# Convolution, top-k token attention and write-back on one core: scatters ordered by image, a semaphore for each image, and the way back two slots sooner

## The reference, cut to what matters

```
xn   = x normalised over each (image, channel) plane
y    = conv 7x7, dilation 5, 32 channels -> 1, of xn, then an affine batch norm
imp  = sigmoid(gelu(y))                      # one value for each pixel
idx  = sorted indices of the 192 largest imp of each image
xs   = xn * imp
tok  = xs at the 192 pixels + position code  # 192 x 32 for each image
t2   = attention (8 heads) + layernorm + feed-forward + layernorm of tok
xs at the 192 pixels := t2
out  = x + xs
```

## Time and profile before

| what | us |
|---|---|
| median of 3 runs (lowest, highest) | 1260.27 (1259.71, 1261.93) |
| profiled execution | 1271.68 |
| its span | 1269.9 |
| PE busy | 962.1 |
| DVE busy | 836.7 |
| ACT busy | 791.3 |
| POOL busy | 615.8 |

### The profile page before, as it was taken

How to read it: one execution, slowest core, us unless ns; L and a number is a source line. 1 busy time by engine, 2 the same in 40 slices (tenths; PEclk the granted TensorE clock), 3 DMA queues, 4 the chain that set the end, 5 groups by cost and what they waited for, 6 DMA issues and landing times.

```text
span 1269.9 us, 21613 instructions
## 1 busy us (share of the span) xinstructions
PE 962.1 (76%) x6440; PEld 739.8 (58%) x6440; DVE 836.7 (66%) x2116; ACT 791.3 (62%) x1938; POOL 615.8 (48%) x845
## 2 busy tenths in 40 slices
PE   1297686678978888888888888887777688488647
PEld 1175564467756665776577666765655466376434
DVE  7143677657856876688778777876677468455523
ACT  1154464457646776677768677867577578478535
POOL 1032332661466366645764475548444663671532
PEclk9599797889989999999999999999889589789855
DMA  9379896855666789878997899776645456447768
GB/s 213 103 229 261 222 266 180 226 127 147 160 154 155 193 229 255 211 214 245 254 234 206 244 246 246 188 208 178 160 109 147 122 123 192 135 118 217 206 186 272
DMA packets 181225, 246.89 MB, mean 194 GB/s; under 512 B 70742, under 2 KB 77142, under 8 KB 181110
## 3 DMA queue, kind: packets, MB, share of 16 engines
q1 hardware_dynamic: 170613, 238.46, 69.3%
q10 hardware_dynamic: 2304, 4.65, 1.7%
q0 software_dynamic: 8192, 2.40, 1.5%
HBM read 123.61 MB, written 121.80 MB: 193 GB/s over the span
## 4 chain that ended last, share of the span: by engine, by line
PE 38%; DVE 18%; issue 11%; DMA 10%; POOL 9%; ACT 8%; SPq 5%; DVEq 0%; POOLq 0%; ACTq 0%
PE cv L541 9%; PE sc L660 6%; PE tr L575 5%; PE pp L673 4%; PE xb L525 4%; PE ms L689 3%; DMA flat<-imp_flat 3%; DVE junk L1133 3%; DVE res L1337 2%; PE ib L588 2%; ACT wgt L855 2%; SPq L351 2%; POOL tok_x L1023 2%; POOL tok_imp L1023 2%; POOL tok_pos L1023 2%
## 5 line engine op out<-in xcount | busy, mean ns | idle before, releaser
L541 PE MATMUL cv<-X,w_conv 128*128 128x330 f32 (+1 forms) x1024 | 300.0, 417 | 19.1 <-POOL X L997 16.9
L855 ACT ACTIVATE wgt<-ib,eps_col,mom 128x440 f32<-128x440 f32 (+1 forms) x256 | 176.9, 697 | 170.2 <-PE ib L588 161.7
L1337 DVE SCALAR_TENSOR_TENSOR res<-tr,mom,wgt 128x440 f32<-128x440 f32 (+1 forms) x192 | 122.7, 644 | 174.9 <-PE tr L575 165.1
L541 PEld LDWEIGHTS cv<-X,w_conv 128*128 128x128 f32 x1024 | 188.2, 200 | 53.2 <-issue 20.1
L1041 POOL TENSOR_SCALAR res<-res,mom 128x440 f32<-128x440 f32 (+1 forms) x152 | 93.4, 617 | 230.3 <-DVE res L1337 229.2
L525 PE MATMUL xb<-cst,X 128*110 128x128 f32 x900 | 150.5, 293 | 71.3 <-ACT xt L821 51.0
L660 PE MATMUL sc<-k_b,qm 128*128 128x192 f32 x768 | 170.1, 346 | 13.5 <-ACT pr L884 5.9
L821 ACT COPY xt<-xb 110x512 f32<-110x512 f32 x225 | 130.6, 581 | 66.7 <-DMA table<-xt 35.2
L525 PEld LDWEIGHTS xb<-cst,X 128*110 128x110 f32 x900 | 103.5, 141 | 97.9 <-ACT xt L821 56.2
L1133 DVE TENSOR_SCALAR_CACHE_REDUCE junk<-flat,th 128x379 bf16<-128x379 f32 x200 | 120.2, 601 | 54.0 <-ACT th L841 53.4
L575 PE MATMUL tr<-cst,rt 110*128 110x110 f32 x720 | 112.0, 283 | 54.7 <-issue 38.0
(11 more groups left out here) (176 smaller groups left out, 1559.0 us busy)
## 6 DMA issues: line engine op xcount, KB each, us to landing
table<-xt SPq DMA_DIRECT2D x240, 224.0 KB
rt<-table SPq DMA_DIRECT2D x240, 224.0 KB, 4.7
out<-res SPq DMA_DIRECT2D x320, 137.5 KB
X<-in_x SPq DMA_DIRECT2D x58, 412.5 KB, 5.8
X<-in_x SPq DMA_DIRECT2D x58, 343.8 KB, 5.3
conv_rows<-cvr SPq DMA_DIRECT2D x64, 188.0 KB
y<-conv_rows SPq DMA_DIRECT2D x64, 165.4 KB
out<-res SPq DMA_DIRECT2D x64, 68.8 KB
```

Of the source, the lines that this page charges most:

```text
L541: last = mm(cv[:, 0:CUT[half]], w_conv[:, 4 * q + z], X[:, m % XI, at0:at0 + CUT[half]], start=z == 0, stop=z == 3)
L855: last = A(wgt[:, n % 2, at0:at0 + w], ib[:, at0:at0 + w], ACT.Identity, scale=mom[:, NB * g + b, 2:3], bias=eps_col[:, 1:2])
L1337: last = v.scalar_tensor_tensor(res[:, first + at0:first + at0 + w], back_bank(g, u)[:, at0:at0 + w], mom[:, NB * g + b, 0:1], wgt[:, n % ...
```

## The change

Three things are changed. The two scatters that POOL issues in one slot are now those of one image (k = b and k = 4 + b), in the order of the images, and each image has its own semaphore `scat[b]`, raised by 16 by each of two DMAs. The load of unit 0 waits for image 0's only, and the loads of the first units that hold rows of images 1, 2 and 3 (7 and 8, 15, 22 and 23) for theirs; the other readers wait for all four. And BACK is SCORES + 40 = 127 instead of 129, so that every instruction of the way back, with its loads, the parts of the importance and the output stores, stands two slots sooner against the rest, and the whole schedule has two slots fewer.

```diff
-        scat = raised("scat", 1, 8 * 16)
+        scat = [raised(f"scat{b}", 1, 2 * 16) for b in range(NB)]
...
-        SCATTER, BACK = SCORES + 36, SCORES + 42
+        SCATTER, BACK = SCORES + 36, SCORES + 40
         IMPB = (BACK - 3, BACK + 1, BACK + 9, BACK + 16)
...
                 n = U * g + u
-                if u == 0:
-                    sp.wait_ge(scat, upto(scat, g))
+                for b in range(NB):
+                    if 4 * max(u - 1, 0) // RQ < b <= (4 * u + 3) // RQ or u == b == 0:
+                        sp.wait_ge(scat[b], upto(scat[b], g))
...
-            def scatter(g, part):
+            def scatter(g, b):
                 pool.wait_ge(t2_ok, upto(t2_ok, g))
-                for k in range(2 * part, 2 * part + 2):
+                for k in (b, NB + b):
                     gp.indirect_dma_start(table[g], bass.IndirectOffsetOnAxis(ap=idx[:, g % 2, 0, k:k + 1], axis=0),
-                                          rb[:, k, :], None).then_inc(scat, 16)
+                                          rb[:, k, :], None).then_inc(scat[b], 16)
...
                 if g >= 2:
-                    dve.wait_ge(scat, upto(scat, g - 2))
+                    for b in range(NB):
+                        dve.wait_ge(scat[b], upto(scat[b], g - 2))
...
                     if g:
-                        dve.wait_ge(scat, upto(scat, g - 1))
+                        for b in range(NB):
+                            dve.wait_ge(scat[b], upto(scat[b], g - 1))
```

## The result

The changed kernel took 1249.52 us (median of 4 runs, 1245.91 to 1252.68) against 1261.1 for the kernel before (1259.71 to 1271.67). The ratio is 0.9864, interval 0.9828 to 0.9899: 1.36% faster, some 17 us, where 9.3 us (0.74%) had been forecast. Two later repeats gave 0.9872 (0.9832 to 0.9911) and 0.9849 (0.9817 to 0.9881). So the direction was right and the size was not. The median of 1249.52 by itself lies inside the range, and the medians of the first runs are only 11.6 apart; but they are of four runs each, and executions of one kernel spread by 10 us and more (e4, the same kernel: 1243.80 to 1257.67).

What follows compares the result with a forecast made beforehand. No engine was taken to bound the whole; the tail was a block of DMA work starting at SP's release. -7.3 + 1.0 - 3.5 + 0.5 = -9.3 us, from 1260.27 to 1251.0 us; range 1245.9 to 1259.5.

Steps and rivals of the forecast that it cites:

- First image's semaphore, end of the last group: End of last group: SP released after the second scatter instead of the eighth, gain 7.3 us (ends 0 and 7.34).
- the store of block 11: End of last group: SP reaches this output store at 1217.3, POOL's unit is finished at 1217.0, so it just fits.
- Two slots fewer: Two more units of work come before the last group's last scatter: +1.0 us (ends 0 and 2).
- The rotation: Middle: the way back's loads move to the quiet slot, the flat load lands sooner: -3.5 us (half of 7.05).
- The new waits: SP's scatter waits: covered in groups 0 to 3, tight in group 6: +0.5 us (ends 0 and +3.2).
- The rule weighed there: SP's traffic can hold up an image's own semaphore; group 6 would pay 3.2 us, making the sum -6.6.
- Rival B: Only the end gains, the flat load waits as before: -5.8 us, 1254.5 us; chance 0.27.
- C: Rival: the end doesn't gain, as the first image's count comes with later scatters; 1258 to 1261 us; chance 0.13.
- D: Rival: slower, the flat load in slot 8 comes later in five groups; +9.7 us, 1270 us; chance 0.10.

Runs made afterwards that it cites:

- e4: The changed kernel again, unaltered, against the kernel before on a fast chip (1267 us); ratio 0.9872, median 1252.1 us.
- e1: Scatters by image with a semaphore each, BACK left at 129, against the kernel before (1267 us); ratio 0.9936, median 1258.7 us.
- e16: The changed kernel once more, unaltered, against the kernel before on a fast chip (1267 us); ratio 0.9849, median 1249.0 us.
- e3: As e1, but SP issues the way back's seven loads early, in slots 125 to 128; against the kernel before, ratio 0.9868, median 1249.9 us.
- e15: The kernel of e3 again, beside e16, against the kernel before (1267 us); ratio 0.9869, median 1252.1 us.
- e13: The kernel before with only the flat load moved, to slot 37 from 38; against the kernel before, ratio 0.9877, median 1252.5 us.
- e14: The kernel before with only the flat load moved, to slot 39 from 38; against the kernel before, ratio 1.0094, median 1279.8 us.
- e2: BACK = 127 alone, with the kernel before's one semaphore and scatter order; against the kernel before, ratio 1.017, median 1287.8 us.
- e12: The changed kernel, unaltered, against the kernel before on a slower chip (1434 us); ratio 0.9941, median 1426.2 us.

## Why the forecast was half of the gain

1. *First image's semaphore, end of the last group: right.* Forecast release 2.08 us after the second scatter, PE idle some 7 us, the store of block 11 just fitting. Traced: 2.07, 6.87, and the store not held. e1 gives 8.1 us (4.8 to 11.3) against 7.3, with the release 0.5 us later than forecast. The block behind was 54.2 us long (1191.89 to the end) instead of 52.4, within what such tails vary (52.1 in e4, 54.0 in e16).
2. *Two slots fewer: +1.0 forecast, too small to be seen.* e3 and e15 keep BACK = 129 and have the time of e4 and e16, within some 4 us. Whether the term is 0, 1 or 2 us stays open.
3. *The rotation: the step that failed, in size.* The mechanism was as forecast: loads in the quiet slot, the waits on the flat load at zero in groups 3 to 7 (0.4 and 0.5 us in the repeats), and compute showed no part in it. But I priced it at half of PE's idle time, -3.5, with the reason that "PE is 78% busy there, so a next limit is near". Neither the wait nor its place was wrong, but the overlap: I took half of it to be absorbed by PE's other work. The busy share of a window doesn't say that. The schedule is a chain of slots, DVE's wait stood in it, and what stands behind started later by the whole wait. Measured directly, by e3 against e1, the term is -8.6 us, some 4 us to either side, for 8.7 us of waits gone. With e1's 8.1 that is 16.7 us, which is the gain (16 to 19 us in three comparisons). e13 and e14 give the same price, 1.1 to 1.2, within their intervals. The 10.5 us of rows 5 are one execution's; in e1's trace groups 3 to 7 wait 9.5 us.
4. *The new waits: +0.5 forecast, no cost in the trace.* SP stood at scatters 42.2 us in all (21.6 before). No run prices this by itself. In group 1 the first image's took longer than at the quiet end, with the second scatter at 533.83 and SP released at 538.90, but the next table write waited for ACT until 544.35, 11.9 us after the group's first scatter, as in the kernel before (11.8). In group 6 the release came after 2.08 us and PE didn't wait for its first unit:

```profile
1118.53 0.92 POOL L1057 DMA_INDIRECT table<-rb,idx  x1 [0.30 <-issue]
...
1120.61 3.14 SPq L396 DMA_DIRECT2D rt<-table  x7
```

The rule weighed there, that a completion counts only after earlier writes of the same DMA engines (the Trainium skill, DMA: Bandwidth & Descriptors, "Queues, rings and completion order"), fits the 5.07 us of group 1 beside the 2.07 and 2.08 us in quiet places. So would scatters that are themselves slower among other traffic, and no run here tells the two apart. The 3.2 us that it would have cost in group 6 didn't come, since the release there took 2.08 us.

Rival B (only the end gains) is refuted by e3 and e4 against e1, C by the release, which came before the last five scatters had even been issued, D by the flat load, on which DVE no longer waits. e2 shows that a longer wait of SP at the scatters, for all eight of them, does cost.

## What to carry to other kernels

Where a row of waits shows a small load on which a serial stage starts, count its whole wait as time, not the share that looks idle on another engine (on the slower chips here it was nearer to half); then look at what stands ahead of it in its queue. Moving one such load by one slot was worth 15 us here, nearly as much as the whole change. And before a consumer is pulled forward past a producer, split what it waits for: the same two slots cost 1.7% with one semaphore (e2), and with four the kernel with them is 0.64% faster than without (e4 and e1).

## What was not expected of the hardware

One kernel takes 1267 us on some chips and 1424 to 1434 on others, and much of the difference is in one place. In the changed kernel on a slow chip (e12, timeline) PE and ACT stand while POOL's gathers go out, and go on only once the last of them has begun:

```profile
634.29 0.31 SPq L396 DMA_DIRECT2D rt<-table  x1
...
646.67 0.92 POOL L1024 DMA_INDIRECT tok_pos<-in_pos,idx  x1 [0.30 <-issue]
...
648.39 0.72 ACT L856 ACTIVATE wgt<-ib,eps_col,mom 128x440 f32<-128x440 f32 x1 [17.21 <-remote]
...
650.23 0.97 PE L576 MATMUL tr<-cst,rt 110*128 110x110 f32 x4 [12.62 <-issue]
```

What they waited for isn't shown. SP had issued a load of the way back at 634.29, but the profile names no releaser for PE (`issue`) and one that it can't place for ACT (`remote`), and from 640 to 646 us the DMA engines were only 7% busy. Between e12 and e4 one interval between two of ACT's copies of the way in, or two neighbouring ones, is 16.0 to 18.0 us longer in each of five groups. That makes some 84 of the 169 us between the two spans; the rest wasn't followed.

On a fast chip (e4) PE goes on turning units between the gathers of the same group, with no stall over 1.3 us:

```profile
591.78 0.57 PE L576 MATMUL tr<-cst,rt 110*128 110x110 f32 x4 [0.62 <-issue]
596.07 0.57 PE L576 MATMUL tr<-cst,rt 110*128 110x110 f32 x4 [0.55 <-issue]
600.11 0.57 PE L576 MATMUL tr<-cst,rt 110*128 110x110 f32 x4
```

Why the chips differ isn't shown. It means that a gain of half a per cent can only be compared among kernels that ran on one chip.
